# Block maxima and exponents for two heads in one instruction, from a score tile of two neighbouring banks

## The reference

```python
scores = jnp.einsum('bhsd,bhjkd->bhsjk', q, kb) * SCALE
scores = jnp.where(diag_mask[None, None], -jnp.inf, scores)   # causal inside the diagonal block
w = jax.nn.softmax(scores.astype(jnp.float32), axis=-1)       # over one block of 32 keys
w = w * include[None, None, :, :, None]                       # blocks up to the query's own
out = jnp.einsum('bhsjk,bhjkd->bhsd', w, vb)
norm = jnp.sum(w, axis=(-2, -1), keepdims=False)[..., None]
return out / (norm + 1e-06)
```

## Time and profile before

| | |
|---|---|
| median of 3 runs | 515.23 us (515.08 to 517.48) |
| span of the profiled execution | 514.7 us; its own time isn't given beside the span, and the median lies 0.5 us above the span |
| TensorE, VectorE, ScalarE, GpSimd busy | 83%, 62%, 35%, 32% of the span |
| mean granted TensorE clock | 0.904 |

### The profile page before, as it was taken

The page is one execution under the profiler, slowest core; times in us unless marked ns, Lnnn a source line. Parts: engine busy times, 40 slices in busy tenths (PEclk is TensorE's granted clock), DMA queues, the critical chain, the costliest instruction groups (busy, mean ns, idle before and its releaser), DMA issues.

```text
span 514.7 us, 10761 instructions
## 1 busy us (share of the span) xinstructions
PE 427.9 (83%) x3616; PEld 396.0 (77%) x3616; DVE 321.2 (62%) x872; ACT 180.3 (35%) x409; POOL 165.4 (32%) x274
## 2 busy tenths in 40 slices
PE   1746399789959995999857997899959999998885
PEld 1734379688849985999757996799959999897775
DVE  4425379839737874688524875488728868656241
ACT  2521025514414342533432324433434344434140
POOL 5320501003704152324521155233523214317162
PEclk9985659969969998999977999799989999899898
DMA  7498943912960079003930039201960110010000
GB/s 184 134 115 172 80 136 90 106 41 81 129 88 3 0 149 114 18 2 104 116 60 3 1 119 105 54 3 46 143 69 2 42 32 3 1 32 10 22 0 22
DMA packets 44078, 33.84 MB, mean 66 GB/s; under 512 B 2981, under 2 KB 41893, under 8 KB 43837
## 3 DMA queue, kind: packets, MB, share of 16 engines
q1 hardware_dynamic: 44028, 33.18, 40.4%
HBM read 23.21 MB, written 9.96 MB: 64 GB/s over the span
## 4 chain that ended last, share of the span: by engine, by line
PE 62%; DMA 19%; SPq 7%; DVE 4%; issue 4%; POOL 2%; ACT 2%; POOLq 0%; DVEq 0%; ACTq 0%
PE X L772 30%; DMA KS<-parts_d 16%; PE PO L866 11%; SPq L419 7%; PE SA L827 3%; PE SB L850 3%; DMA parts_d<-parts 2%; PE X L795 2%; PE SA L830 1%; PE SA L829 1%; PE SA L828 1%; PE SB L853 1%; DMA raw<-wqkv 1%; PE SB L852 1%; PE SB L851 1%
## 5 line engine op out<-in xcount | busy, mean ns | idle before, releaser
L667 DVE TENSOR_REDUCE nmax<-SA 128x12 f32<-128x384 f32 x128 | 66.8, 554 | 73.8 <-PE SA L830 73.6
L866 PE MATMUL PO<-VB,PT 128*128 128x68 f32 x768 | 98.5, 280 | 0.0
L866 PEld LDWEIGHTS PO<-VB,PT 128*128 128x128 f32 x768 | 93.5, 197 | 3.0 <-issue 2.7
L600 POOL TENSOR_TENSOR hid<-gsil,ups 128x256 f32<-128x256 f32 x64 | 47.3, 742 | 123.5 <-DVE ups L756 121.4
L827 PE MATMUL SA<-KS,QS 96*128 96x256 bf16 x128 | 41.9, 328 | 50.3 <-DMA KS<-parts_d 48.9
L772 PE MATMUL X<-x_h,wgu_h 128*128 128x256 f32 x256 | 78.0, 305 | 0.7 <-ACT sbc L512 0.5
L772 PE MATMUL X<-x_l,wgu_h 128*128 128x256 f32 x256 | 73.2, 286 | 0.0
L772 PE MATMUL X<-x_h,wgu_l 128*128 128x256 f32 x256 | 72.9, 285 | 0.0
L491 ACT ACTIVATE PT<-SB 128x384 f32<-128x384 f32 x128 | 56.0, 489 | 47.4 <-PE SB L853 36.6
L606 POOL TENSOR_TENSOR hid_l<-hid,hid_h 128x256 fp32r<-128x256 f32 x64 | 46.4, 732 | 39.1 <-ACT hid_h L523 38.9
L827 PEld LDWEIGHTS SA<-KS,QS 96*128 96x128 bf16 x128 | 13.9, 108 | 57.7 <-issue 30.1
(11 more groups left out here) (118 smaller groups left out, 988.4 us busy)
## 6 DMA issues: line engine op xcount, KB each, us to landing
parts_d<-parts SPq DMA_DIRECT2D x16, 384.0 KB, 2.9
QS<-parts_d SPq DMA_DIRECT2D x48, 128.0 KB, 7.2
KS<-parts_d SPq DMA_DIRECT2D x48, 128.0 KB, 8.0
x_sb<-x SPq DMA_DIRECT2D x8, 256.0 KB, 11.0
raw<-wgu SPq DMA_DIRECT2D x8, 256.0 KB, 3.9
xres<-x SPq DMA_DIRECT2D x8, 256.0 KB, 2.8
out<-x SPq DMA_DIRECT2D x16, 128.0 KB, 1.8
max_d<-mt_sb SPq DMA_DIRECT2D x8, 192.0 KB, 10.0
```

Source lines behind the costliest of these rows:

```text
L600: nc.gpsimd.tensor_tensor(hid[k % 2][:, :], gsil[k % 2][:, :], ups[k % 2][:, :], ALU.mult)\
L667: nc.vector.tensor_reduce(nmax[:, 0:NC_, h], SA[h % 2][:, 0:SC] .rearrange("p (c s) -> p c s", s=BS), AX.X, ALU.max, negate=True)\
L866: last = pe.matmul(o[:, dst:dst + PW], PT[k % 2][:, n, src:src + P], v[:, t, 2 * k + n, :], start=True, stop=True)
```

## The change

SA and SB become one tile each of [128, 2, 512], two neighbouring banks. One instruction of VectorE takes the maxima of both heads of a unit (768 columns, 24 blocks), one of ScalarE the exponents of both. The semaphores count units instead of heads: TensorE fills both banks of a unit after waiting once for the previous unit's maxima or exponents, and signals once, with the last product of the second head. The number of products and the orders are the same.

```diff
-        SA = [pb(f"SA{n}") for n in range(2)]
-        SB = [pb(f"SB{n}") for n in range(2)]
+        SA = ctx.enter_context(nc.psum_tensor("SA", [P, 2, 512], F32))
+        SB = ctx.enter_context(nc.psum_tensor("SB", [P, 2, 512], F32))
...
-                        sp.wait_ge(b_ready, b.times(NH, -NH))
+                        sp.wait_ge(b_ready, b.times(8, -8))
...
-                    for h in (2 * k, 2 * k + 1):
-                        act.wait_ge(b_ready, b.times(NH, h + 1))
-                        nc.scalar.activation(PT[k % 2][:, h % 2, :], SB[h % 2][:, 0:SC], ACT.Exp, scale=SCALE)\
-                            .then_inc(exp_done, 1)
+                    act.wait_ge(b_ready, b.times(8, k + 1))
+                    nc.scalar.activation(PT[k % 2][:, :, :], SB[:, :, 0:SC], ACT.Exp, scale=SCALE).then_inc(exp_done, 1)
...
-                    pool.wait_ge(a_max, b.times(NH, NH))
+                    pool.wait_ge(a_max, b.times(8, 8))
...
-                    for h in (2 * k, 2 * k + 1):
-                        dve.wait_ge(a_ready, b.times(NH, h + 1))
-                        nc.vector.tensor_reduce(nmax[:, 0:NC_, h], SA[h % 2][:, 0:SC]
-                                                .rearrange("p (c s) -> p c s", s=BS), AX.X, ALU.max, negate=True)\
-                            .then_inc(a_max, 1)
+                    dve.wait_ge(a_ready, b.times(8, k + 1))
+                    nc.vector.tensor_reduce(nmax[:, 0:NC_, 2 * k:2 * k + 2].rearrange("p c h -> p h c"),
+                                            SA[:, :, 0:SC].rearrange("p h (c s) -> p h c s", s=BS),
+                                            AX.X, ALU.max, negate=True).then_inc(a_max, 1)
...
+                    if k or not (b.trip is None and b.base == 0):
+                        pe.wait_ge(a_max, b.times(8, k))
                     for h in (2 * k, 2 * k + 1):
-                        if h >= 2 or not (b.trip is None and b.base == 0):
-                            pe.wait_ge(a_max, b.times(NH, h - 1))
-                        bank = SA[h % 2]
+                        bank = SA[:, h % 2, :]
...
-                        pe.matmul(bank[:, S:SC], ident_b, mask_a, start=False, stop=True)\
-                            .then_inc(a_ready, 1)
+                        last = pe.matmul(bank[:, S:SC], ident_b, mask_a, start=False, stop=True)
+                    last.then_inc(a_ready, 1)
...
+                    if k or not (b.trip is None and b.base == 0):
+                        pe.wait_ge(exp_done, b.times(8, k))
                     for h in (2 * k, 2 * k + 1):
-                        if h >= 2 or not (b.trip is None and b.base == 0):
-                            pe.wait_ge(exp_done, b.times(NH, h - 1))
-                        bank = SB[h % 2]
+                        bank = SB[:, h % 2, :]
...
-                    pe.wait_ge(exp_done, b.times(NH, 2 * k + 2))
+                    pe.wait_ge(exp_done, b.times(8, k + 1))
```

More of the change, by code:

```diff
@@ L852, in _ @@
                         pe.matmul(bank[:, S:SC], key[:, h, P:S], q[:, h, P:S], start=True, stop=False)
-                        pe.matmul(bank[:, S:SC], ident_b, mask_b, start=False, stop=True)\
-                            .then_inc(b_ready, 1)
+                        last = pe.matmul(bank[:, S:SC], ident_b, mask_b, start=False, stop=True)
+                    last.then_inc(b_ready, 1)
                 if stage == "PV":
```

## The result

The changed kernel is slower: 526.27 us, median of 4 executions (523.84 to 529.24), against 516.25 us of the kernel before in the same comparison (515.08 to 517.48). The ratio is 1.0197, 95% interval 1.0150 to 1.0244, so 10 us, or 8 to 13. The forecast was 6.8 us more, 522.0, range 518.5 to 527. The profiled execution took 523.84 us with a span of 521.8. Before, the profiled span was 514.7.

A forecast was written before the change was run, and what follows sets the result against it. TensorE was taken as the bound (83% busy, 62% of the chain), waiting mainly for operand stacks by DMA. 5.15 us in batch 1's stage A plus 1.64 of short stalls made 6.8 more: 522.0 us, range 518.5 to 527.

The forecast's parts named there:

- The ring: Batch 1's stage A (scores for maxima): TensorE and VectorE alternate, pair period 2.28 us against 1.37, 5.15 us lost.
- Its way on: After batch 0's last exponent-score stage, SP issues batch 2's operand stack 5.15 us later; first score product 109.8, not 104.62.
- Batch 0's stage A: Its maxima stage grows 6.4 us, hidden in TensorE's 8.39 us idle time before batch 1's; 2 us to spare.
- The short stalls: A few other pairs lacking covering work between them: TensorE waits 0.13 to 0.42 us each, 1.64 us in all.
- The loop's body: Distance from stack to stack in the loop unchanged within 1 us.
- The sum: Whole kernel: 5.15 + 1.64 = 6.8 us more, giving 522.0 us.
- rival A: Batch 0's exponent-score stage: clock rises late, one or two pairs cost 2 to 3.6 us more, 525; chance 0.12.
- From the span to the median: Whole kernel: median 515.23 lies 0.5 us above the profiled span 514.7, so span 521.5 becomes 522.0.
- B: All over the kernel: half of the 128 pairs lose 0.22 us, 14 us more, 536; chance 0.05.
- C: Low-clock stretches after six stack waits all shorten to 3.2 us, giving 6.6 us back, 515.4; chance 0.08.
- D: VectorE: merging saves up to 0.17 us a pair, 10.9 us, 504 if VectorE were the bound; chance 0.02.

The follow-up runs named there:

- the experiment that merges there alone: Kernel before with the maxima merged only in batch 1's stage A (8 of 64 units), all else per head: 1.0133, 6.9 us over before.
- the second comparison: The changed kernel run once more, nothing else altered, against the kernel before: 1.0174 (1.0135 to 1.0214), 9 us over.
- the changed kernel with increments: Changed kernel plus two or three idle semaphore increments on VectorE behind each merged reduction: 1.0206 against the kernel before.
- the coupled kernel: Kernel before, still one instruction per head, but TensorE waits before a pair for both heads of the pair before: 1.0168, 8.7 us over before.
- two kernels with a part of the change: Changed kernel with batch 1's stage A per head, 1.0165 against before; kernel before with only the maxima merged, 1.0252.
- the three other padded kernels: Idle VectorE increments added to the changed kernel (1.0206), to it with batch 1's stage A per head (1.0051), and there with fewer (1.0110), all against before.

## Why the prediction was right

*The ring.* Right in place and size: period 2.28 foreseen, 2.30 measured; 5.15 us to B0.0 foreseen, 5.3 measured (14.9 - 9.6). The reduction of 768 columns took 0.96 (0.95), the exponents 0.81 (0.80): the slope per column held, and what doesn't grow with the columns was paid once. Shown by the experiment that merges there alone.

*Its way on.* Right: SP's issue came 5.6 us later counted from the stage's start; TensorE waited for the stack as long as before, 17.0 us from the last B to A2.0 against 16.9. A2.0 was foreseen at 109.8 and came at 109.04, in an execution that was 1.3 us ahead at A1.0.

*Batch 0's stage A.* Right, and shown: 1.74 us of idle time left of 8.39, with 2 foreseen:

```profile
62.11 0.40 PE L824 MATMUL SA<-KS,QS 96*128 96x256 bf16 x1 [1.74 <-DMA KS<-parts_d]
```

*The short stalls.* Most came where they were foreseen. In the changed kernel, B3.1 (to the earlier trace rows) and B7.1 (to the earlier trace rows) start right behind the exponents:

```profile
216.12 0.80 ACT L490 ACTIVATE PT<-SB 128x768 f32<-128x768 f32 x1
216.98 0.28 PE L847 MATMUL SB<-QS,KS 120*128 120x256 bf16 x1 [0.24 <-ACT PT L490]
...
431.33 0.28 PE L847 MATMUL SB<-QS,KS 120*128 120x256 bf16 x1 [0.52 <-ACT PT L490]
```

Before A2.3 and B1.6 TensorE idles 0.13 and 0.18 us (0.23 and 0.20 foreseen), and A4.6 to A4.7 was covered, as foreseen. Before B5.1 and A7.6 it shows no idle time in any of the three traces, before B6.1 it has 0.21 and 0.17 us in two of them, and before B7.4, where the delay was taken to cost nothing, it idles 0.43 us. The sum of the idle times in the first trace is 1.5 us, near the 1.64 foreseen.

What failed is their price. The traces' last part, from A1.0 on, is 8.4, 9.2 and 8.7 us longer than before; the ring is 5.3 of it each time and the stretch with the jump 0.9, 1.1 and 0.5, so 2.2, 2.8 and 2.9 us are left where 1.64 was counted. And the exponents alone cost 4.1 us (2.3 to 5.9) where 1.3 was counted. Why isn't shown. A loss of clock to the stalls isn't what these traces have: the changed kernel is at the low level for 11 to 14 us longer, but all of that lies ahead of B0.0, in batch 0's stage A with the idle time behind it and in the ring. Behind B0.0 it is 61 to 64 us, as before (64), more in some stretches (5.9 us in place of 3.9 from batch 6's first A, 4.6 in place of 3.0 from batch 7's) and less in another (9.0 in place of 13.0 from A5.0 to B4.7).

How a microsecond at the low level counts can be read from the kernel before itself: in one comparison its fastest execution of 22 took 513.62 us at a mean clock of 0.910, one of the slowest 520.79 at 0.891; with spans 2 us shorter that is 92 and 113 us low, 7.2 us for 21, a third of a microsecond each. A line through all 22 gives the same (0.34); through the executions of the two other comparisons 0.35 and 0.19.

*The loop's body.* "Unchanged within 1 us" held, but for another reason than foreseen in the second trip: 0.9 us of the 7.1 come from VectorE's gap behind the jump, which no row of before showed. In the kernels with a part of the change that stretch was up to 6 us longer than before.

*The sum.* 6.8 us foreseen. Between the spans of the profiled executions it is 7.1, 7.5 and 7.8 us, between the medians 10.0 (8 to 13), and 9 in the second comparison. So the mechanism carries the shorter executions, and about 3 us of the median's 10 lie in the longer ones, which the sum didn't have. That 526.27 still lies in the range owes something to chance: the range was widened upwards for rival A, which no trace of the changed kernel shows.

*From the span to the median.* I took what lies around the span to be 0.5 us, from the median. Each execution of later comparisons has both numbers, and the difference is 2.0 us (523.84 to 521.8). So the traced execution of before must have been one of about 516.7 us, and the forecast for a profiled execution should have been 523.5, where it is (523.84). Between the medians this step cancels: there 516.25 in place of 515.23 moved before by 1.0 us, and the change itself came out 3.2 us dearer than foreseen. The four executions took 523.84, 524.22, 528.32 and 529.24 us at mean clocks of 0.895, 0.889, 0.887 and 0.887. By the third of a microsecond above, the 10 us more at the low level of the longest would be 3.4 of its 5.4 us. That the longer ones are rival A, a late clock, is what the changed kernel with increments showed in one trace; for the changed kernel itself it is argued from the mean clock alone.

*The rivals.* A: real in one kernel's trace, and with more behind it (11 us in that stretch, not 2 to 3.6). B (every pair stalls, 536): fell, the loop's stretches are within 1.1 us. C (the clock gives it back): fell; behind B0.0 the changed kernel has as much low clock as before. D (pays as meant): fell; 64 pairs saved 5.6 us of VectorE's time and nothing of the kernel's. The Trainium skill's sentence that unsaturated engines which make bubbles elsewhere may have the work done sooner with smaller instructions (page "Perfetto Trace Analysis", section "Optimizing Scalar/DVE Operations") fits this case, and the coupled kernel adds what it doesn't say: over half of the ring's loss (0.53 of 0.93 us) came from the shared wait, with the instructions as small as before.

*Still open.* Why the short stalls cost more than their own length, with the exponents above all; why the coupled kernel and the one with the maxima alone lose more of the clock behind B0.0 than the whole change does; what exactly in the layout of VectorE's instructions makes none, one or two gaps; and the trace of a changed kernel's long execution.

## What to carry to other kernels

Merging two small instructions over two buffers takes away the double buffering between them: before doing it, find the stretch where producer and consumer alternate with nothing else between, and price the new ring as producer of both + consumer of both + handoffs. Such a stretch costs only if the engine isn't waiting for something later anyway, which the idle time in front of the next stage tells. In an order written by hand, the safe form keeps per-head waits and instructions in that stretch; here even that gained nothing over the kernel before, since the engine relieved had time to spare.

## What was not expected of the hardware

- Right behind the jump back to the loop's start VectorE stood still for 1.9 to 2.3 us (changed), 4.7 to 5.0 us (two kernels with a part of the change), 2.3 us (before with 64 more semaphore increments), 2.0 to 2.5 us (the three other padded kernels) or not at all (before, and those kernels whose VectorE has 696 or 697 instructions ahead of the jump and 378 or 379 in the trip), with nothing to wait for in the profile. TensorE has 5.0 us of idle time at its own jump in the kernel before, and 4.6 to 5.6 in the other traces:

```profile
272.94 1.11 PE L795 MATMUL X<-cst,o_sb 128*128 128x128 f32 x4 [5.01 <-issue]
```

  The transfers show what this goes with. Besides the kernel's own queue the profile has two of kind "instruction", q8 and q14. In the 5.6 us behind VectorE's jump that hold the two gaps of the kernel with batch 1's stage A per head, q14 has two packets (number, MB, share), and in the 3.2 us behind the jump of the kernel before no packet runs at all:

```profile
q14 instruction: 2, 0.02, 0.9%
```

```profile
DMA packets 0, 0.00 MB, mean 0 GB/s; under 512 B 0, under 2 KB 0, under 8 KB 0
```

  It is so in all 14 traces: each of the nine with a gap has a q14 packet about 1 us behind VectorE's jump, the two with a double gap have a second before it ends, and the five without a gap have none between 266 and 390 us. Behind TensorE's jump q8 has two. So the engine most likely waits, though that is argued from the times alone, for its own instructions to be loaded again; the profile doesn't name the engine that a packet is for. A kernel that differs by a few instructions per trip can so differ by 1 to 5 us in that stretch.
- With TensorE busy without a gap the granted clock stayed at 1.2 GHz for all of a stretch of 26 us in one execution, where 2.7 us of it were at that level in another with the same products.
- The kernel before itself spreads over 7 us from one execution to the next (513.62 to 520.79), and its mean granted clock with it (0.910 to 0.891). In span x 2 x (1 - clock) that is 92 to 113 us at the low level. A trace that is a few microseconds longer than another, with 7 us more at the low level (as with the exponents merged only, or the merging in batch 1's stage A), lies inside this spread; the 116 us of the coupled kernel and the 126 of the one with the maxima alone lie above it.
